# Two cross attentions: query scores directly behind mask and key scores, input transposes and query projection one period ahead

## The chip, the cores and the metric

The kernel runs on one core of a Trainium2 chip. The metric is device time in microseconds from the first to the last work of the program. Five engines work beside each other, each through its own queue in order: TensorE (PE, matrix multiplies), VectorE (DVE), ScalarE (ACT), GpSimd (POOL) and SyncE (SP, which here only issues transfers). They wait for one another by semaphores.

## The reference, cut to what matters

A decoder of two layers over 16 sequences of 256 rows of 256 numbers. Each layer is a mixer, a cross attention and a mixture of experts. The change touches only the two cross attentions. What one computes (16 heads of 16 numbers; the one of layer 0 has a mask):

```
q = x @ Wq.T + bq;  k = ctx @ Wk.T + bk;  v = ctx @ Wv.T + bv     # ctx has 256 rows as well
scores = einsum('bhqd,bhkd->bhqk', q, k) / sqrt(16)
scores = where(mask == 0, -1e9, scores)                           # layer 0 only
out = einsum('bhqk,bhkd->bhqd', softmax(scores), v)
x = layernorm(x + out @ Wo.T + bo)
logits = x @ router.T                                             # then top 2 of 7, or top 4 of 32
```

## The kernel before, in words

`xattn_stage` is built once for each layer. One sequence n is a unit of work; it passes through stages, and a *period* p works on several sequences at once: q = p is in its first pass over the scores, k = p-1 and l = p-2 in the second pass and the output, r = p-3 in the routing, and a = p+1 is being projected. `at(n, part, g)` issues a part if the sequence exists. The order in each engine's queue is written out by hand in the loops `for p in PERIODS`.

The softmax needs the maximum of each row first. So the scores are computed twice, in eight groups g of four heads by 128 rows:

- `query_scores(q, g)` (Q below; `x_ps<-x_kpack,x_qpack`, four matmuls on 48 of the array's rows) gives scores with the queries on the partitions. VectorE's `maxima(q, g)` takes the row maxima, in layer 0 with four custom operations that also add the mask (L1170), in layer 1 with one reduction (L1174). There is one buffer in PSUM, so Q of the next group waits for these maxima.
- `turn_maxima` (L912, `x_nmx`) transposes the finished maxima of all groups into the first bank of the same buffer; ScalarE's `keep_maxima` takes them negated, and SP's `pack_maxima` copies them as a 49th row beside the queries. Q of the next sequence waits until ScalarE has taken them.
- `key_scores(k, g)` (K; `x_ps<-x_qpack,x_kpack`, 49 rows) gives the transposed scores less the maximum. In layer 0 two matmuls with the mask (M, L892) go first. ScalarE's `weights` takes the exponential (L1068). `weigh` (W, L931, 16 matmuls) multiplies it with the values, `turn_output` (L943) transposes the result, VectorE's `scaled` divides it (L1181, L1183), `turn_scaled` (L851) and `output` (L954) project it, VectorE's `add_output` (L1191) adds it and takes the statistics, `normalize` (L206) ends it.

The queries and keys of sequence a are projected by `project_queries` and `project_keys` (L857), with the values' `project_values` (L883); the rows must first be transposed by `turn_in` (L851). All of these share one bank. ScalarE's `keep_queries` and `keep_keys` take them as a rounded part (`qh`, `kh`) and in full; GpSimd's `low_queries` (L803) and `low_keys` (L808) make the rest (`ql`, `kl`); SP packs both with six transfers each into `qpack` and `kpack`, which hold three sequences. GpSimd waits at each of these operations until VectorE is at a certain group of maxima: `beside_maximum`, group 2 for `low_queries`, 4 for `low_keys`, 5 for `add_bias` (L816).

The routing of r is `turn_rows` (L851), `route` (L970), VectorE's `take_logits`, `choose` (L1215 to L1226), `one_hot` (L1232 to L1240) and `weigh_experts` (L1246 to L1255), then `rank` on TensorE (L979 to L982) and `place` on VectorE. In layer 1 GpSimd also sends the rows out by indirect transfers (L826), four behind `low_queries` and four at the end of the period.

Of the kernel before, what the change touches and what calls it, by code (L numbers as in the profile page):

```python
# [7 lines left out]
F32 = mybir.dt.float32  # L8
# [604 lines left out]
def xattn_stage(nc, st, d, layer):  # L613
# [15 lines left out]
    PACKS = 3  # L629
    LOWEST = -3e38  # L630
    PACK_DMAS = 12
    GROUPS = QUADS * TB
    SLOTS = (0, 2, 1, 3)
    with ExitStack() as ctx:
# [58 lines left out]
        cx_loaded = [sem(f"cx_loaded{u}") for u in range(U)]  # L693
        pack_loaded = [sem(f"pack_loaded{u}") for u in range(PACKS)]
        max_loaded = [sem(f"max_loaded{u}") for u in range(PACKS)]
# [21 lines left out]

        PERIODS = range(-1, B + 4)

# [4 lines left out]
        def _(sp):  # L724
# [22 lines left out]

            def pack(dst, n, part, src):
                for m in range(KC):
                    lo = 64 * m + DH * part  # L750
                    sp.dma_start(dst[lo:lo + DH, n % PACKS].bitcast(F32),
                                 src[:, m, :].bitcast(F32)).then_inc(pack_loaded[n % PACKS], 16)

            def pack_queries(n):
                if n >= PACKS:
                    sp.wait_ge(st_ready, GROUPS * (n - PACKS + 1))
                sp.wait_ge(qh_ready, n + 1)
                pack(qpack, n, 0, qh)
                pack(qpack, n, 1, qh)
                sp.wait_ge(ql_ready, n + 1)  # L760
                pack(qpack, n, 2, ql)

            def pack_keys(n):
                if n < PACKS:
                    sp.wait_ge(ones_ready, n + 1)
                sp.wait_ge(kh_ready, n + 1)
                pack(kpack, n, 0, kh)
                pack(kpack, n, 2, kh)
                sp.wait_ge(kl_ready, n + 1)
                pack(kpack, n, 1, kl)  # L770

# [20 lines left out]
        def _(pool):  # L792
# [5 lines left out]
            def low_queries(n):  # L798
                pool.wait_ge(qh_ready, n + 1)
                if n:  # L800
                    pool.wait_ge(pack_loaded[(n - 1) % PACKS], 16 * PACK_DMAS * ((n - 1) // PACKS + 1))
                beside_maximum(n - 1, 2)
                pool.tensor_tensor(ql[:], qf[:], qh[:].bitcast(F32), ALU.subtract).then_inc(ql_ready, 1)  # L803

            def low_keys(n):
                pool.wait_ge(kh_ready, n + 1)
                beside_maximum(n - 1, 4)
                pool.tensor_tensor(kl[:], kf[:], kh[:].bitcast(F32), ALU.subtract).then_inc(kl_ready, 1)  # L808
# [37 lines left out]
        def _(pe):  # L846
# [53 lines left out]
            def query_scores(n, g):  # L900
                if g == 0:
                    pe.wait_ge(pack_loaded[n % PACKS], 16 * PACK_DMAS * (n // PACKS + 1))
                    if n:
                        pe.wait_ge(nmT_ready, n)
                if n or g:
                    pe.wait_ge(max_ready, GROUPS * n + g)
                scores(QUERY, n, g, qpack, kpack, 3 * DH, False).then_inc(s_ready, 1)
# [76 lines left out]

            for p in PERIODS:
                a, q, k, l, r = p + 1, p, p - 1, p - 2, p - 3
                at(l, key_scores, 6)
                at(l, weigh, 2)
                at(a, turn_in)
                at(k, turn_maxima)  # L990
                at(l, key_scores, 7)
                at(q, query_scores, 0)

                at(a, project_queries)
                at(r, turn_rows)
                at(q, query_scores, 1)

                at(l, weigh, 3)
                at(k, key_scores, 0)
                at(r, route)  # L1000
                at(q, query_scores, 2)

                at(k, key_scores, 1)
                at(a, project_keys)
                at(l, turn_output)
                at(q, query_scores, 3)

                at(k, key_scores, 2)
                at(k, weigh, 0)
                at(q, query_scores, 4)  # L1010

                at(k, key_scores, 3)
                at(a, project_values)
                at(l, turn_scaled)
                at(q, query_scores, 5)

                at(k, key_scores, 4)
                at(l, output)
                at(r, rank)
                at(q, query_scores, 6)  # L1020

                at(k, key_scores, 5)
                at(k, weigh, 1)
                at(q, query_scores, 7)
            if masked:
# [4 lines left out]
        def _(act):  # L1030
# [8 lines left out]
            def keep_queries(n):  # L1039
                act.wait_ge(q_ready, n + 1)  # L1040
                if n:
                    act.wait_ge(pack_loaded[(n - 1) % PACKS], 16 * PACK_DMAS * ((n - 1) // PACKS + 1))
                for c in range(KC):
                    act.activation(qf[:, c, :], bank(PROJ)[:, c, :], ACT.Identity, bias=bqk[:, 0, c:c + 1], scale=1.0)
                for c in range(KC):
                    ins = act.activation(qh[:, c, :], bank(PROJ)[:, c, :], ACT.Identity, bias=bqk[:, 0, c:c + 1], scale=1.0)
                ins.then_inc(qh_ready, 1)

            def keep_keys(n):
                act.wait_ge(k_ready, n + 1)  # L1050
                for c in range(KC):
                    act.activation(kf[:, c, :], bank(PROJ)[:, c, :], ACT.Identity, bias=bqk[:, 1, c:c + 1], scale=1.0)
# [39 lines left out]

            for p in PERIODS:
                a, k, l, r = p + 1, p - 1, p - 2, p - 3
                at(l, weights, 6)
                at(l, keep_values, 2)
                at(a, keep_rows)
                at(k, keep_maxima)
                at(l, weights, 7)

                at(a, keep_queries)
                at(r, keep_normal)

                at(l, keep_values, 3)
                at(k, weights, 0)

                at(k, weights, 1)
                if not masked:
                    at(r, gates)
                at(a, keep_keys)  # L1110

                at(k, weights, 2)
                at(k, keep_values, 0)

                at(k, weights, 3)
                if masked:
                    at(r, gates)
                at(l, keep_scaled)

                at(k, weights, 4)  # L1120

                at(k, weights, 5)
                at(k, keep_values, 1)

        @block.vector
        def _(dve):
# [151 lines left out]
            for p in PERIODS:  # L1278
# [15 lines left out]
                at(q, maxima, 6)  # L1294
                at(l, add_output)
# [994 lines left out]
```

## Time and profile before

| | |
|---|---|
| median of 3 runs | 3034.13 us (3027.97 to 3039.84) |
| the profiled execution: its own time, from its first to its last instruction (the span) | 3014.5 us; what lies around the span has no row |
| mean granted clock of TensorE over the span | 0.908 |
| busy: TensorE, VectorE, ScalarE, GpSimd | 2479.8, 1989.7, 1085.6, 829.1 us |
| cross attention of layer 0 | about 580 to 1068 us of the span |
| cross attention of layer 1 | about 2309 to 2790 us of the span |

Busy time is the sum of the durations of an engine's instructions. Matmuls overlap one another, so for TensorE the distances between the starts of groups tell more than the durations. "idle <- X" behind a row is the time in which the engine had nothing to run before it, and who released it. PEld are the weight loads that go before matmuls.

### The profile page before, as it was taken

What the parts mean: (1) busy time and instruction counts of PE and PEld (TensorE: products, weight loads), DVE (VectorE), ACT (ScalarE), POOL (GpSimd) and SP (SyncE); (2) the same over time, 40 slices, a digit from 0 to 9 for tenths busy, and PEclk for the clock granted to TensorE, in tenths of its full rate; (3) what the DMA queues carried; (4) which work ended last, traced back from release to release, by engine and by line L of the source; (5) the groups of instructions that cost most, each with busy time, mean ns of one, the idle gap of its engine ahead of it and who ended that gap; (6) DMA issues with size and microseconds to landing.
All of it is one profiled execution on the core that took longest, in us unless ns stands there. A gap on an engine that the chain in (4) does not pass through costs nothing. (4 is left out here: it accounts for less than half of the span.)

```text
span 3014.5 us, 50862 instructions
## 1 busy us (share of the span) xinstructions
PE 2479.8 (82%) x17441; PEld 2072.9 (69%) x17442; DVE 1989.7 (66%) x5320; ACT 1085.6 (36%) x1953; POOL 829.1 (28%) x1118
## 2 busy tenths in 40 slices
PE   3877887679999969999999999977675898887680
PEld 3666666546666569999999999966564566665670
DVE  5888888356776656566666666546553587886458
ACT  2333433235555522221222222212263555553450
POOL 0010001111111136223523213015311144444664
PEclk8998999879999979999999999988887898996895
DMA  1112213253544120001302202112102656550436
GB/s 56 50 49 67 78 49 117 46 78 68 110 68 75 23 91 35 28 31 64 112 31 70 70 28 70 34 52 58 35 0 45 83 99 125 78 76 3 128 110 246
DMA packets 170608, 206.04 MB, mean 68 GB/s; under 512 B 21061, under 2 KB 148847, under 8 KB 170480
## 3 DMA queue, kind: packets, MB, share of 16 engines
q1 hardware_dynamic: 139680, 154.58, 22.9%
q0 software_dynamic: 15360, 23.63, 2.7%
q10 hardware_dynamic: 15440, 26.22, 2.5%
q8 instruction: 69, 1.13, 0.2%
q14 instruction: 59, 0.48, 0.1%
HBM read 95.42 MB, written 77.20 MB: 57 GB/s over the span
## 5 line engine op out<-in xcount | busy, mean ns | idle before, releaser
L1538 PE MATMUL m_gu<-m_x_hi,m_w_hi 128*128 128x256 f32 x1632 | 461.1, 283 | 17.9 <-issue 10.4
L1538 PE MATMUL m_gu<-m_x_hi,m_w_lo 128*128 128x256 f32 x1632 | 457.7, 280 | 0.0
L1538 PE MATMUL m_gu<-m_x_lo,m_w_hi 128*128 128x256 f32 x1632 | 457.2, 280 | 0.0
L1575 ACT ACTIVATE m_sg<-m_gu 128x256 f32<-128x256 f32 x408 | 156.8, 384 | 668.7 <-PE m_gu L1538 668.7
L1609 DVE TENSOR_TENSOR m_h<-m_sg,m_gu 128x256 f32<-128x256 f32 x408 | 171.7, 421 | 286.6 <-ACT m_sg L1575 284.0
L1068 ACT ACTIVATE x_pt<-x_ps 128x1024 f32<-128x1024 f32 x256 | 262.0, 1024 | 224.5 <-PE x_ps L896 221.3
L1538 PEld LDWEIGHTS m_gu<-m_x_hi,m_w_hi 128*128 128x128 f32 x1632 | 308.9, 189 | 22.0 <-issue 11.8
L1538 PEld LDWEIGHTS m_gu<-m_x_lo,m_w_hi 128*128 128x128 f32 x1632 | 308.8, 189 | 0.0
L1538 PEld LDWEIGHTS m_gu<-m_x_hi,m_w_lo 128*128 128x128 f32 x1632 | 308.6, 189 | 0.0
L1170 DVE CUSTOM_DVE_ANT_0 x_ps<-x_ps,x_mb 128x256 f32<-128x256 f32 x512 | 201.7, 457 | 118.6 <-PE x_ps L896 118.5
L1527 PE MATMUL m_yp<-m_w_hi,m_h_hi 128*128 128x256 f32 x816 | 240.1, 294 | 5.1 <-DVE m_h_lo L1611 4.6
L1527 PE MATMUL m_yp<-m_w_lo,m_h_hi 128*128 128x256 f32 x816 | 230.2, 282 | 0.0
L1527 PE MATMUL m_yp<-m_w_hi,m_h_lo 128*128 128x256 f32 x816 | 229.3, 281 | 0.0
L1611 DVE TENSOR_TENSOR m_h_lo<-m_h,m_h_hi 128x256 fp32r<-128x256 f32 x408 | 198.9, 488 | 14.3 <-DVE m_h_hi L1610 0.4
L1174 DVE TENSOR_REDUCE x_nmx<-x_ps 128x4 f32<-128x1024 f32 x128 | 156.0, 1218 | 74.4 <-PE x_ps L896 73.9
L369 PE MATMUL rw_ps<-rw_mix,rw_fk 128*128 128x256 f32 x512 | 146.2, 456 | 56.8 <-DVE rw_mix L477 56.8
L896 PE MATMUL x_ps<-x_kpack,x_qpack 48*128 48x256 f32 x1024 | 135.3, 344 | 67.0 <-DVE x_nmx L1174 36.6
L369 PEld LDWEIGHTS rw_ps<-rw_mix,rw_fk 128*128 128x128 f32 x512 | 118.5, 235 | 82.0 <-DVE rw_mix L477 60.8
L896 PEld LDWEIGHTS x_ps<-x_kpack,x_qpack 48*128 48x128 f32 x1024 | 82.5, 198 | 125.2 <-DVE x_nmx L1174 55.3
L1527 PEld LDWEIGHTS m_yp<-m_w_hi,m_h_hi 128*128 128x128 f32 x816 | 154.0, 189 | 10.3 <-DVE m_h_lo L1611 7.4
L1455 POOL CAST m_w_hi<-raw 128x256 fp32r<-128x256 f32 x168 | 64.3, 432 | 343.4 <-DMA raw<-in_L_ffn_w_down 338.9
L188 POOL TENSOR_TENSOR rw_rstd<-rw_var,eps 128x2 f32<-128x2 f32 x48 | 11.2, 234 | 524.6 <-DVE rw_var L201 524.6
(314 smaller groups left out, 5718.2 us busy)
## 6 DMA issues: line engine op xcount, KB each, us to landing
yt<-zero SPq DMA_DIRECT2D x8, 2048.0 KB, 10.3
x_qpack<-x_qh SPq DMA_DIRECT2D x128, 128.0 KB, 4.0
x_kpack<-x_kh SPq DMA_DIRECT2D x128, 128.0 KB, 4.2
m_yr<-yt SPq DMA_DIRECT2D x16, 1024.0 KB, 13.3
m_x<-xs SPq DMA_DIRECT2D x36, 256.0 KB
ys<-m_y SPq DMA_DIRECT2D x35, 256.0 KB, 2.2
xs<-zero SPq DMA_DIRECT2D x8, 1072.0 KB, 5.9
m_x<-xs SPq DMA_DIRECT2D x32, 268.0 KB, 3.2
```

What stands on the lines that cost most here:

```text
L188: pool.tensor_tensor(rstd[:, u, :], var[:, u, :, 1], st.eps[:, 0:TB], ALU.add).then_inc(eps_added, 1)
L369: ins = pe.matmul(bank(u, m // 2)[:, m % 2, :], fk[:, c, m * P:m * P + P], mix[:, u, 0, c, :], start=(c == 0), stop=(c == KC - 1))
L896: ins = pe.matmul(bank(first + k // 2)[:, k % 2, :], left[here, n % PACKS, blk, t * P:t * P + P], moving[here, n % PACKS, blk, :], start=n ...
L1068: act.activation(pt[:, j % 2, t].rearrange("p k q -> p (k q)"), ps[:, KEY:KEY + 2].rearrange("p k q -> p (k q)"), ACT.Exp, scale=SCALE).th ...
L1170: ins = dve.tensor_tensor_reduce(row, row, mb[:, 0, t, :], op0=ALU.add, op1=ALU.max, scale=1.0, scalar=LOWEST, accum_out=nmx[:, n % U, t, ...
L1174: ins = dve.tensor_reduce(nmx[:, n % U, t, 0:HEADS].rearrange("p (m q b) -> p m q b", m=2, q=QUADS)[:, :, j, :], ps[:, QUERY:QUERY + 2].re ...
L1455: pool.tensor_copy(w_hi[:, b, n, piece], raw[:, n, piece]).then_inc(hi_ready, 1)
L1527: ins = pe.matmul(yp[:, n, 0:D], hp[:, m, n * P:n * P + P], wp[2][:, m, :], start=(m == 0 and k == 0), stop=(m == FC - 1 and k == 2))
L1538: ins = pe.matmul(gu[:, m % 4, n, :], wp[n][:, c, m * P:m * P + P], xp_[:, c, :], start=(c == 0 and k == 0), stop=(c == KC - 1 and k == 2))
L1575: act.activation(sg[:, m % 4, :], gu[:, m % 4, 0, :], ACT.Silu).then_inc(silu_ready, 1)
L1609: s.do(dve.tensor_tensor(h[:, m % 4, :], sg[:, m % 4, :], gu[:, m % 4, 1, :], ALU.mult))
L1611: dve.tensor_tensor(h_lo[:, m, :], h[:, m % 4, :], h_hi[:, m, :].bitcast(F32), ALU.subtract).then_inc(h_ready, 1)
```

## The change

On TensorE, `query_scores` of group g now stands directly behind `key_scores` of another group in all eight blocks of a period (before, other work stood between some of them). `turn_in` and `project_queries` work on b = p+2 instead of a = p+1, so there is one more period at the start. `turn_maxima` moves from the beginning of the next period to the end of its own. `project_keys`, `route`, `turn_output`, `turn_scaled`, `output`, `rank` and `project_values` change their blocks. The orders on ScalarE and VectorE follow; on VectorE `choose` moves behind `scaled`, and `values` ahead of maxima 5. Since queries are now packed in another period than keys, the one semaphore for both packs becomes two with six transfers each, and the waits on it are split; `keep_keys` and `low_keys` get a wait for the keys' pack of the sequence before.

```diff
-    PACK_DMAS = 12
+    PACK_DMAS = 6
...
-        pack_loaded = [sem(f"pack_loaded{u}") for u in range(PACKS)]
+        qpack_loaded = [sem(f"qpack_loaded{u}") for u in range(PACKS)]
+        kpack_loaded = [sem(f"kpack_loaded{u}") for u in range(PACKS)]
...
-        PERIODS = range(-1, B + 4)
+        PERIODS = range(-2, B + 4)
...
             def low_keys(n):
                 pool.wait_ge(kh_ready, n + 1)
+                if n:
+                    pool.wait_ge(kpack_loaded[(n - 1) % PACKS], 16 * PACK_DMAS * ((n - 1) // PACKS + 1))
                 beside_maximum(n - 1, 4)
...
             def query_scores(n, g):
                 if g == 0:
-                    pe.wait_ge(pack_loaded[n % PACKS], 16 * PACK_DMAS * (n // PACKS + 1))
+                    pe.wait_ge(qpack_loaded[n % PACKS], 16 * PACK_DMAS * (n // PACKS + 1))
+                    pe.wait_ge(kpack_loaded[n % PACKS], 16 * PACK_DMAS * (n // PACKS + 1))
...
             for p in PERIODS:
-                a, q, k, l, r = p + 1, p, p - 1, p - 2, p - 3
+                b, a, q, k, l, r = p + 2, p + 1, p, p - 1, p - 2, p - 3
                 at(l, key_scores, 6)
+                at(q, query_scores, 0)
                 at(l, weigh, 2)
-                at(a, turn_in)
-                at(k, turn_maxima)
+                at(r, turn_rows)
+
                 at(l, key_scores, 7)
-                at(q, query_scores, 0)
-
-                at(a, project_queries)
-                at(r, turn_rows)
                 at(q, query_scores, 1)
+                at(a, project_keys)
+                at(r, route)
+
+                at(k, key_scores, 0)
+                at(q, query_scores, 2)
                 at(l, weigh, 3)
-                at(k, key_scores, 0)
-                at(r, route)
-                at(q, query_scores, 2)
 
                 at(k, key_scores, 1)
-                at(a, project_keys)
+                at(q, query_scores, 3)
+                at(a, project_values)
                 at(l, turn_output)
-                at(q, query_scores, 3)
 
                 at(k, key_scores, 2)
+                at(q, query_scores, 4)
                 at(k, weigh, 0)
-                at(q, query_scores, 4)
+                at(l, turn_scaled)
 
                 at(k, key_scores, 3)
-                at(a, project_values)
-                at(l, turn_scaled)
                 at(q, query_scores, 5)
+                at(l, output)
+                at(b, turn_in)
 
                 at(k, key_scores, 4)
-                at(l, output)
+                at(q, query_scores, 6)
+                at(b, project_queries)
                 at(r, rank)
-                at(q, query_scores, 6)
 
                 at(k, key_scores, 5)
+                at(q, query_scores, 7)
                 at(k, weigh, 1)
-                at(q, query_scores, 7)
+                at(q, turn_maxima)
...
             def keep_keys(n):
                 act.wait_ge(k_ready, n + 1)
+                if n:
+                    act.wait_ge(kpack_loaded[(n - 1) % PACKS], 16 * PACK_DMAS * ((n - 1) // PACKS + 1))
...
                 at(l, weights, 6)
                 at(l, keep_values, 2)
-                at(a, keep_rows)
-                at(k, keep_maxima)
+                at(r, keep_normal)
+
                 at(l, weights, 7)
-
-                at(a, keep_queries)
-                at(r, keep_normal)
-
+                at(a, keep_keys)
+
+                at(k, weights, 0)
                 at(l, keep_values, 3)
-                at(k, weights, 0)
 
                 at(k, weights, 1)
                 if not masked:
                     at(r, gates)
-                at(a, keep_keys)
 
                 at(k, weights, 2)
                 at(k, keep_values, 0)
+                at(l, keep_scaled)
 
                 at(k, weights, 3)
                 if masked:
                     at(r, gates)
-                at(l, keep_scaled)
+                at(b, keep_rows)
 
                 at(k, weights, 4)
+                at(b, keep_queries)
 
                 at(k, weights, 5)
                 at(k, keep_values, 1)
+                at(q, keep_maxima)
...
                 at(q, maxima, 0)
                 at(r - 1, place)
                 at(q, maxima, 1)
+                at(q, maxima, 2)
                 at(r, take_logits)
-                at(q, maxima, 2)
-                at(r, choose)
                 at(q, maxima, 3)
                 at(l, scaled)
+                at(r, choose)
                 at(q, maxima, 4)
+                at(a, values)
+                at(q, maxima, 5)
                 at(r, one_hot)
-                at(q, maxima, 5)
-                at(a, values)
+                at(q, maxima, 6)
                 at(r, weigh_experts)
-                at(q, maxima, 6)
                 at(l, add_output)
                 at(q, maxima, 7)
```

## Rows read from the trace of the kernel before

**Rows 1.** Stretches (length; busy PE, PEld, DVE, ACT, POOL; clock, DMA share, GB/s); layer 0, 1

```profile
685.27:978.34 293.07, 291.41 (x2321) 185.86 (x2322) 205.08 (x1033) 163.76 (x276) 51.88 (x55) 1.00 0.47 82
2424.31:2739.03 314.72, 278.11 (x2308) 198.68 (x2308) 256.08 (x575) 174.74 (x291) 146.55 (x150) 0.90 0.55 87
2424.31:2449.02 24.71, 21.69 (x195) 15.67 (x195) 21.29 (x49) 14.91 (x26) 8.76 (x9) 1.00 0.53 98
2473.94:2500.88 26.94, 24.38 (x197) 17.56 (x196) 21.61 (x49) 15.08 (x26) 12.81 (x13) 0.88 0.58 93
```

**Rows 2.** TensorE in order of time, layer 0 (start us, us, engine, line, operation)

```profile
828.93 1.04 PE L943 MATMUL x_ps<-ident,x_o 128*128 128x128 f32 x8
829.90 0.50 PE L896 MATMUL x_ps<-x_kpack,x_qpack 48*128 48x256 f32 x4
...
831.30 1.07 PE L931 MATMUL x_ps<-x_pt,x_vp 128*32 128x256 f32 x16
832.30 0.50 PE L896 MATMUL x_ps<-x_kpack,x_qpack 48*128 48x256 f32 x4
832.74 0.60 PE L892 MATMUL x_ps<-x_mb,identb 128*128 128x512 bf16 x2
833.27 0.50 PE L896 MATMUL x_ps<-x_qpack,x_kpack 49*128 49x256 f32 x4
833.70 1.99 PE L883 MATMUL x_ps<-x_wv,x_cx 128*128 128x256 f32 x8
835.53 0.60 PE L851 MATMUL x_ps<-ident,x_aq 128*128 128x128 f32 x4
836.06 0.51 PE L896 MATMUL x_ps<-x_kpack,x_qpack 48*128 48x256 f32 x4
```

**Rows 3.** Weight loads in order of time where K and Q adjoin, layer 0

```profile
818.47 0.20 PEld L912 LDWEIGHTS x_ps<-ident,x_nmx 128*128 128x128 f32 x2 [0.38 <-DVE x_nmx L1170]
...
819.27 0.30 PEld L896 LDWEIGHTS x_ps<-x_qpack,x_kpack 49*128 49x128 f32 x4 [0.42 <-issue]
...
819.50 0.31 PEld L896 LDWEIGHTS x_ps<-x_kpack,x_qpack 48*128 48x128 f32 x4
...
819.94 0.19 PEld L857 LDWEIGHTS x_ps<-x_xT,x_wqk 128*128 128x128 f32 x1
```

**Rows 4.** VectorE in order of time, end of a period, layer 0

```profile
840.15 0.43 DVE L1170 CUSTOM_DVE_ANT_0 x_ps<-x_ps,x_mb 128x256 f32<-128x256 f32 x1 [0.83 <-PE x_ps L896]
...
843.44 0.41 DVE L1170 CUSTOM_DVE_ANT_0 x_ps<-x_ps,x_mb 128x256 f32<-128x256 f32 x1
```

**Rows 5.** VectorE's choose, then GpSimd's low_keys, layer 0

```profile
827.74 0.24 DVE L1220 MAX8 x_mx<-x_lg 128x8 f32<-128x8 f32 x2
...
828.42 0.14 DVE L1226 TENSOR_TENSOR x_tmp<-x_mx 128x2 f32<-128x2 f32 x1
...
832.96 1.27 POOL L808 TENSOR_TENSOR x_kl<-x_kf,x_kh 128x512 fp32r<-128x512 f32 x1 [5.30 <-PE x_ps L896]
```

**Rows 6.** GpSimd's low_queries, low_keys and VectorE's cast, layer 1

```profile
2535.30 1.27 POOL L803 TENSOR_TENSOR x_ql<-x_qf,x_qh 128x512 fp32r<-128x512 f32 x1 [2.22 <-PE x_ps L896]
...
2541.55 1.29 POOL L808 TENSOR_TENSOR x_kl<-x_kf,x_kh 128x512 fp32r<-128x512 f32 x1
2541.96 0.93 DVE L1232 CAST rows<-x_ix 128x8 f32<-128x8 uint32 x1
```

**Rows 7.** VectorE and GpSimd in the tail of layer 1

```profile
2748.86 1.83 DVE L1217 TENSOR_TENSOR x_lg<-x_sc,ebias 128x64 f32<-128x64 f32 x1
...
2749.31 1.29 POOL L816 TENSOR_TENSOR x_y<-rows,x_rows 128x512 f32<-128x512 f32 x1
```

**Rows 8.** Stretches of VectorE's work, layer 1: maxima 0, place, 1; choose; weigh_experts to add_output

```profile
2529.49:2533.68 4.19, 4.19 (x37) 2.92 (x37) 3.95 (x9) 2.70 (x7) 2.91 (x3) 1.00 0.29 74
2536.60:2538.63 2.03, 2.03 (x20) 1.73 (x18) 1.65 (x10) 1.31 (x4) 1.60 (x2) 1.00 1.02 310
2546.83:2551.47 4.64, 2.87 (x44) 1.41 (x42) 4.24 (x14) 2.28 (x3) 0.00 (x0) 0.95 1.13 174
```

More of the change, by code:

```diff
@@ L746, in load_context, with pack @@
                     sp.dma_start(cx[:, n % U], ctx_v[:, :, S * n:S * n + S]).then_inc(cx_loaded[n % U], 16)
-            def pack(dst, n, part, src):
+            def pack(dst, n, part, src, loaded):
                 for m in range(KC):
@@ L751, in pack @@
                     sp.dma_start(dst[lo:lo + DH, n % PACKS].bitcast(F32),
-                                 src[:, m, :].bitcast(F32)).then_inc(pack_loaded[n % PACKS], 16)
+                                 src[:, m, :].bitcast(F32)).then_inc(loaded[n % PACKS], 16)
             def pack_queries(n):
@@ L757, in pack_queries @@
                 sp.wait_ge(qh_ready, n + 1)
-                pack(qpack, n, 0, qh)
-                pack(qpack, n, 1, qh)
+                pack(qpack, n, 0, qh, qpack_loaded)
+                pack(qpack, n, 1, qh, qpack_loaded)
                 sp.wait_ge(ql_ready, n + 1)
-                pack(qpack, n, 2, ql)
+                pack(qpack, n, 2, ql, qpack_loaded)
             def pack_keys(n):
@@ L766, in pack_keys @@
                 sp.wait_ge(kh_ready, n + 1)
-                pack(kpack, n, 0, kh)
-                pack(kpack, n, 2, kh)
+                pack(kpack, n, 0, kh, kpack_loaded)
+                pack(kpack, n, 2, kh, kpack_loaded)
                 sp.wait_ge(kl_ready, n + 1)
-                pack(kpack, n, 1, kl)
+                pack(kpack, n, 1, kl, kpack_loaded)
             def pack_maxima(n):
@@ L800, in low_queries @@
                 if n:
-                    pool.wait_ge(pack_loaded[(n - 1) % PACKS], 16 * PACK_DMAS * ((n - 1) // PACKS + 1))
+                    pool.wait_ge(qpack_loaded[(n - 1) % PACKS], 16 * PACK_DMAS * ((n - 1) // PACKS + 1))
                 beside_maximum(n - 1, 2)
@@ L1041, in keep_queries @@
                 if n:
-                    act.wait_ge(pack_loaded[(n - 1) % PACKS], 16 * PACK_DMAS * ((n - 1) // PACKS + 1))
+                    act.wait_ge(qpack_loaded[(n - 1) % PACKS], 16 * PACK_DMAS * ((n - 1) // PACKS + 1))
                 for c in range(KC):
@@ L1093, in _ @@
             for p in PERIODS:
-                a, k, l, r = p + 1, p - 1, p - 2, p - 3
+                b, a, q, k, l, r = p + 2, p + 1, p, p - 1, p - 2, p - 3
                 at(l, weights, 6)
                 at(l, keep_values, 2)
-                at(a, keep_rows)
-                at(k, keep_maxima)
+                at(r, keep_normal)
                 at(l, weights, 7)
-                at(a, keep_queries)
-                at(r, keep_normal)
+                at(a, keep_keys)
+                at(k, weights, 0)
                 at(l, keep_values, 3)
-                at(k, weights, 0)
                 at(k, weights, 1)
```

## The prediction, made before the changed kernel had run

> **What bounds the kernel now.** First I read the busy time of the engines in the two cross attention stages, by stretches [rows 1]. Of eleven full periods of the first stage (each one sequence of 256 rows; 293.07 us, so 26.64 us a period) TensorE is busy 291.41 us at full clock, VectorE 205.08: TensorE bounds it. In the second stage a clean period takes 24.71 us, and VectorE, busy 21.29 us of it, is the tighter engine. [...] The twelve full periods take 314.72 us, 26.23 on average.
>
> A busy TensorE says little about its peak, so next I read its order of time [rows 2]. Its slots are the distances between starts: transposing the output 0.97 us (O8, 828.93 to 829.90), weighing 1.00 (W, from 831.30), query scores 0.44 (Q, 832.30), mask 0.53 (M), key scores 0.43 (K), a projection 1.83 (P, from 833.70), four small transposes 0.53 (T, 835.53 to 836.06). For routing (R, eight matmuls) I take O8's 1.0, for the five placement matmuls of `rank` .2, both estimates. There is no gap in the first stage but before the transpose of the maxima.
>
> Third, the one place of the old order where K and Q stand side by side [rows 3]: weight loads start at 819.27 (K), 819.50 (Q), 819.94 (projection). The pair takes 0.67 us, not 0.43 + 0.44 = 0.87.
>
> **The change, part by part.** *Pairs.* In the masked stage K is followed by Q once a period today, and eight times after: 7 x 0.20 = 1.4 us less TensorE work a period [rows 2, 3]. The period's TensorE work goes from 26.64 - 0.27 (the wait before the maxima's transpose, 0.80 between it and T instead of 0.53; its idle shows at 818.47 [rows 3]) = 26.37 to 24.95. In the unmasked stage Q and the next K already adjoin where no other work stands between, seven times a period, so only one pair is won: 0.2 us.
>
> *Where the saving goes.* `turn_maxima` needs all eight maxima. Today the next period's first M, K, W and `turn_in` lie between Q7 and it (2.5 us); after, one W (1.0). I count from Q6, layer 0. TensorE: Q .44 + P 1.83 + rank .2 + M .53 + K .23 + Q .44 + W 1.0 = 4.67 us. VectorE: .6 until the scores are read (GpSimd, which waits for the same scores, starts .66 behind Q4: 832.30 and 832.96 [rows 2, 5]; VectorE follows its work without a gap there), maxima 6 and `add_output` 3.29 (adjoining today: 840.15 to 843.44), `weigh_experts` about .56 (three tiny operations like 828.42's), maxima 7 until its transpose is released 1.67 (the same point a period before: 818.47 + 26.64 = 845.11): 6.12 us [rows 3, 4]. So TensorE stands 1.45 us, where it stood 0.27.
>
> *The middle of the period.* I lay the new order out by those slots, T=0 at the first M. Q2 falls at 7.51, Q3 at 9.78 (waits .07 for maxima 2), then P and O8 end at 13.02. `scaled` now precedes `choose` on VectorE and has to wait for O8: 13.16, ends 14.22 (its reciprocal and two products stand 1.06 apart from the next work in VectorE's order of time). `choose` takes .84, its last operation (828.42) begins .68 into it [rows 5], at 14.90. Meanwhile Q4 at 13.78 lets GpSimd's `low_keys` go .66 later (1.27 long [rows 5]): 14.44 to 15.71. The two overlap; today they don't. What does an overlap cost? Today a cast of 8 elements starts at 2541.96 and ends at 2542.89, just behind GpSimd's `low_keys` that ran from 2541.55 to 2542.84 [rows 6], where 828.42's kind takes .14 to .2. And in the tail of layer 1 a subtraction-sized VectorE operation with two inputs in SBUF took 1.83 us and ended when GpSimd's 2749.31 operation did [rows 7]. 828.42 also has two SBUF inputs. No row shows it blocked; the bounds are nothing and .8 us (until 15.77). I take the upper, since the nearest row is [rows 7].
>
> [...]
>
> Then maxima 4 start at 15.77 (else 15.06), Q5 1.67 later at 17.44 (16.73; TensorE would be there at 16.51), Q6 at Q5 + 1.83 + .53 + .44 + .76 = 21.0 (20.29), the transpose of the maxima at Q6 + 6.12 = 27.12 (26.41), and the next period .27 later: 27.39 us (26.68) against 26.64. So +.75 (+.04) a period. Eleven full periods: +8.3 (+.4). The first and last periods lack `choose` or projections; by the same walk they give back about 1. **Layer 0: +7 (-1) us.**
>
> *Layer 1, the same walk* with maxima that stand 1.14 apart when VectorE has them ready. Slots of VectorE: the two first maxima with `place` 4.19, so `place` 1.91; `choose` 2.03; `weigh_experts`, maxima 6 and `add_output` 4.64 [rows 8]. From the transpose of the maxima to Q0 stays about .93. The new waits of VectorE: place ends at 4.22, maxima 1 at 5.36; but Q2 is behind P, R and K0 (now that both stand in one block): 6.27, so maxima 2 start at 6.87: 1.5 us idle. Q3 at 8.14, O8 ends at 11.38, `scaled` waits until 11.52 (nearly 1.9 us behind maxima 3) and `choose` can't fill that, being behind it: 12.57. Its addition with two SBUF inputs comes .8 in, 13.37. GpSimd's `low_queries` starts about .68 behind Q2 (.66 in layer 0), four indirect DMAs follow, and `low_keys` starts 6.25 after it (2535.30, 2541.55 [rows 6]): 13.20 to 14.49. The addition waits until then: choose ends 15.54 (unblocked 14.60). Maxima 4, then Q5 at 16.81 (15.87), where TensorE is at 13.81; later it waits 2.3 more for the maxima's transpose. `add_bias` .66 behind Q5 runs to 18.74 (17.80) and holds back only the cast (.2); today it waits for `low_keys` [rows 6], and I take the same .75 for the later addition of `one_hot`, which today runs beside `add_bias`: `one_hot` shrinks by 1.4, to about 1.7. Q6 19.84 (18.90), maxima 6 from 20.44 (19.50), + 4.63 + 1.25 = transpose at 26.32 (25.38), next period .36 later: 26.68 (25.74) against 24.8, so +1.8 (+.9). Twelve periods: +22 (+10); the periods without projections or routing give back 3.5.
>
> *Clock.* Layer 1's twelve periods average 26.23 us where a clean one takes 24.8: 17 us in all, above all stretches at 1.2 GHz (the average clock is .90 [rows 1]). Today TensorE stands before Q6, Q7 and the maxima's transpose with no projection between; the new order waits more, but with a projection behind each of Q5 and Q6, so the waits are spread. I take a third, 6 us, back; bounds 0 and 17. **Layer 1: +22 - 3.5 - 6 = +12 (0).**
>
> *Hidden.* `turn_in` and `project_queries` a period ahead issue the same instructions and six DMAs; the first set runs while TensorE waits for the first key pack to land. The query packs start earlier on SP, ahead of the key packs, so nothing is queued behind them longer. ScalarE's and GpSimd's new waits for the last key pack are for one that landed a period ago (ScalarE is idle 9.8 of 24.71 us [rows 1]). `keep_queries` between weights 4 and 5 delays weights 5 by .5 us; M of the next period comes 1.3 us later. `pack_maxima` gains 2 us. Were that cover gone, each would cost its own length, .6 to 1.6 us a period.
>
> **Sum.** The profiled execution has a span of 3014.5 us; the runs' median, 3034.1, lies 19.6 above it, which I leave alone. 3034.1 + 7.3 + 12 = 3053 us. Around .5% (15 us) is what can be told from no change.
>
> **Rivals.**
> [...]
> *The saving is kept* (.10), the other side: if the VectorE work from Q6 to the transpose is hidden, TensorE's 24.95 us is the period. It decides at one point, a chain of less than 4.7 us there instead of 6.12. Against it: each term is measured. 11 x 1.42 + 1 + 3 for layer 1 = -20: 3014.
> *The clock falls oftener* (.13): more waiting in layer 1 puts 1.2 GHz into each of twelve periods at 2.2 us: 26 us instead of the 11 that the forecast leaves: 3053 + 15 = 3068. For it: TensorE stands 5 us of 26.7 instead of about 3. Against: the spread, and layer 0's full clock [rows 1] with stands shorter than layer 1's.
>
> **How the numbers follow.** Forecast .52, own range 3041 to 3064. With the rivals at .25, .10 and .13, the range 3026 to 3070 leaves out the kept saving and the worst clock. Slower by over .5% (above 3049): .34 from the forecast and .12 from the clock, .46. Faster (below 3019): .10 and .02 from no collision with all clock regained: .12. The same: .42.
>
> **What would show it.** M, K, Q to the next start in 1.20 us in layer 0; the transposes of the maxima 27.4 us apart (26.7 without the collision), with a wait of about 1.4 us for VectorE; L1226 taking .9 instead of .14; in layer 1, distances of 26.7, L1217 at about 1.2, L1232 and L1239 short, VectorE idle before maxima 2 and before L1181. It is wrong if the wait at L912 is short, if those two stay at .14 and .23, or if the clock in layer 1 changes much.

## The result, and the profile after

The changed kernel takes 3078.21 us (median of 4 runs, 3062.62 to 3086.43), the kernel before 3033.28 beside it: 1.015 times as long, with a 95% interval of 1.0107 to 1.0193. The forecast was 3053 with a range of 3026 to 3070: the direction was right, and the size outside the range. The names and operations are those of before; lines of `xattn_stage` stand 3 to 6 lines further down (L912 is now L916, L896 L899, L1170 L1176, L1174 L1180, L1217 L1223, L1226 L1232).

The span and clock of the profiled execution:

```profile
core 0: 3067.9 us, clock 0.900
```

Layer 0, TensorE in order of time; these answer to [rows 2]:

```profile
854.66 0.59 PE L895 MATMUL x_ps<-x_mb,identb 128*128 128x512 bf16 x2
855.18 0.50 PE L899 MATMUL x_ps<-x_qpack,x_kpack 49*128 49x256 f32 x4
855.52 0.40 PE L899 MATMUL x_ps<-x_kpack,x_qpack 48*128 48x256 f32 x4
855.85 1.07 PE L935 MATMUL x_ps<-x_pt,x_vp 128*32 128x256 f32 x16
...
865.13 0.50 PE L899 MATMUL x_ps<-x_kpack,x_qpack 48*128 48x256 f32 x4 [0.62 <-DVE x_nmx L1176]
...
874.70 0.44 PE L916 MATMUL x_ps<-ident,x_nmx 128*128 128x128 f32 x2 [1.45 <-DVE x_nmx L1176]
```

Mask, keys, queries to the next start take 1.19 us (854.66 to 855.85), the forecast's 1.20 against 1.40 before. The transpose of the maxima waits 1.45 us for VectorE, the forecast's 1.45 against 0.27. The first line below is VectorE's last operation of `choose`, the second GpSimd's `low_keys`; they answer to [rows 5]:

```profile
862.73 0.80 DVE L1232 TENSOR_TENSOR x_tmp<-x_mx 128x2 f32<-128x2 f32 x1
...
862.23 1.28 POOL L811 TENSOR_TENSOR x_kl<-x_kf,x_kh 128x512 fp32r<-128x512 f32 x1 [4.86 <-PE x_ps L899]
```

An operation on two elements of each partition, 0.14 us long before, takes 0.80 and ends when GpSimd's does: the collision of the forecast is there. Yet the transposes of the maxima stand only 26.91 us apart (847.79 to 874.70), not 27.39, and the 15 distances of layer 0 (632.60 to 1031.86) sum to 399.26 us against 396.02: the layer lost 3 us, not 7. Of these 3, one period (792.48 to 820.87, 28.39 us at a clock of 0.94) has 1.5; the other full periods add 0.27 each, and the second distance of the layer gives back 1.2 (24.67 against 25.89).

Layer 1, by stretches (columns as in [rows 1]): all 15 distances between transposes of the maxima, a long one, and one at full clock.

```profile
2363.26:2786.10 422.84, 355.74 (x2792) 249.76 (x2792) 289.78 (x644) 209.25 (x353) 158.28 (x162) 0.87 0.45 78
2492.16:2526.09 33.93, 28.96 (x196) 20.68 (x196) 21.46 (x49) 14.76 (x25) 12.76 (x13) 0.75 0.40 73
2646.81:2672.84 26.03, 21.93 (x195) 15.78 (x196) 20.09 (x49) 14.43 (x25) 12.71 (x13) 1.00 0.46 74
```

The same for the unchanged kernel, profiled a second time for this study (e11 below):

```profile
2356.80:2753.57 396.77, 345.87 (x2819) 243.19 (x2819) 287.30 (x644) 216.25 (x360) 158.14 (x162) 0.91 0.49 83
2590.79:2619.89 29.10, 24.73 (x197) 17.59 (x196) 19.60 (x48) 15.27 (x26) 12.28 (x13) 0.87 0.45 68
2619.89:2645.15 25.26, 22.15 (x196) 15.77 (x196) 20.03 (x49) 14.86 (x26) 12.74 (x13) 1.00 0.52 76
```

Layer 1 lost 26 us. A period at full clock is 26.03 us long against 25.26 here and 24.71 in [rows 1]. The mean clock is 0.87 against 0.91. Cut into stretches of 0.3 us, this layer of the changed kernel has a granted clock of 1.00 in 1019 of 1409 and of 0.50 in 361 (without a break from 2493.50 to 2502.50 us), e11 in 1065 and 234 of 1322: two levels, full and half, and few stretches with a mean between them. So 2 x 0.13 x 422.84 = 110 us are at half clock against 2 x 0.09 x 396.77 = 71. Where the prediction and the expectations give a clock in GHz, they mean the 0.50; no run shows a clock in GHz. Over the last twelve distances, changed kernel and e11:

```profile
2438.52:2786.10 347.58, 292.78 (x2301) 205.90 (x2301) 247.07 (x575) 169.15 (x286) 146.26 (x150) 0.87 0.44 78
2427.20:2753.57 326.37, 283.32 (x2308) 199.96 (x2308) 245.73 (x575) 173.30 (x291) 146.18 (x150) 0.91 0.47 83
```

These are some 90 and 59 us at half clock; [rows 1] have 2 x 0.10 x 314.72 = 63 for the first trace of the kernel before.

What TensorE does before the clock falls shows in a period at full clock. Behind each of these rows stands its wait; the last two lines are VectorE and GpSimd, answering to [rows 7]:

```profile
2663.38 0.50 PE L899 MATMUL x_ps<-x_kpack,x_qpack 48*128 48x256 f32 x4 [1.64 <-DVE x_nmx L1180]
...
2672.84 0.44 PE L916 MATMUL x_ps<-ident,x_nmx 128*128 128x128 f32 x2 [2.13 <-DVE x_nmx L1180]
...
2660.95 0.22 DVE L1223 TENSOR_TENSOR x_lg<-x_sc,ebias 128x64 f32<-128x64 f32 x1
...
2662.03 1.26 POOL L811 TENSOR_TENSOR x_kl<-x_kf,x_kh 128x512 fp32r<-128x512 f32 x1 [1.16 <-remote]
```

Two waits of 1.6 and 2.1 us stand in such a period, as forecast (it had 3.0 before Q5 and 2.3; the first is shorter since the addition L1223 takes 0.22 and is over before `low_keys` begins). In a period in which TensorE is late by a stretch at half clock the two do meet:

```profile
2510.33 1.31 DVE L1223 TENSOR_TENSOR x_lg<-x_sc,ebias 128x64 f32<-128x64 f32 x1
...
2510.26 1.29 POOL L811 TENSOR_TENSOR x_kl<-x_kf,x_kh 128x512 fp32r<-128x512 f32 x1
```

That happens four times (at 2510, 2543, 2576 and 2744 us), and these are the four longest periods, 33.93, 31.54, 31.02 and 30.78 us. In this trace that collision meets only periods that are late already. It is not what makes them long: in e6 below the addition takes 0.22 to 0.23 us throughout, and yet three full periods there are 31.3 to 31.7 us long; and in e7 it takes 1.41 us (at 2459.12) in a period of 26.90 us at full clock.

The waits over the twelve last distances (us in total, times, the longest), changed kernel:

```profile
DVE x_nmx L1180 <- PE x_ps L899: 58.8, 42, 4.4
...
PE x_ps L916 <- DVE x_nmx L1180: 30.2, 13, 3.1
...
PE x_ps L899 <- DVE x_nmx L1180: 22.9, 13, 2.7
```

and the kernel before (e11):

```profile
DVE x_nmx L1174 <- PE x_ps L896: 29.4, 39, 3.3
...
PE x_ps L896 <- DVE x_nmx L1174: 22.7, 27, 1.8
...
PE x_ps L912 <- DVE x_nmx L1174: 4.6, 7, 1.2
```

TensorE waits 53 us for maxima instead of 27, and VectorE 59 us for scores instead of 29. (With VectorE's waits for which the profile finds no releaser, which it calls "remote", 2.7 and 14.0 us, VectorE's are 62 and 43; more of these at e11.) Both engines stand more: neither is the bound of this order, their handing over is.

Between the two spans (3067.9 and 3030.3 in e11) the 37.6 us divide so: until the first transpose of layer 0 1.3, layer 0 3.3, from its last to the first of layer 1 1.9, layer 1 26.1, what follows 5.1. The medians lie some 7 us further apart than the two profiled spans; no trace shows where.

### The profile page after: what moved, and what is told of

The parts are those of the page before. It is cut to its first block and busy times, and to the rows that moved or that the text cites. A ratio compares the mean times of both kernels' runs of the same rounds, so it can differ in the third digit from the quotient of the medians.

```text
span 3067.9 us, 50898 instructions
## 1 busy us (share of the span) xinstructions
PE 2483.1 (81%) x17441; PEld 2084.1 (68%) x17442; DVE 1987.7 (65%) x5320; ACT 1081.6 (35%) x1953; POOL 829.7 (27%) x1118
## 5 line engine op out<-in xcount | busy, mean ns | idle before, releaser
L1176 DVE CUSTOM_DVE_ANT_0 x_ps<-x_ps,x_mb 128x256 f32<-128x256 f32 x512 | 201.6, 456 | 113.6 <-PE x_ps L899 113.6
L1180 DVE TENSOR_REDUCE x_nmx<-x_ps 128x4 f32<-128x1024 f32 x128 | 156.1, 1219 | 115.8 <-PE x_ps L899 106.5
L899 PE MATMUL x_ps<-x_kpack,x_qpack 48*128 48x256 f32 x1024 | 122.2, 319 | 61.3 <-DVE x_nmx L1180 31.1
L1533 PEld LDWEIGHTS m_yp<-m_w_hi,m_h_lo 128*128 128x128 f32 x816 | 153.8, 189 | 0.0
L1533 PEld LDWEIGHTS m_yp<-m_w_lo,m_h_hi 128*128 128x128 f32 x816 | 153.6, 188 | 0.0
```

What stands on the lines that cost most here:

```text
L899: ins = pe.matmul(bank(first + k // 2)[:, k % 2, :], left[here, n % PACKS, blk, t * P:t * P + P], moving[here, n % PACKS, blk, :], start=n ...
L1176: ins = dve.tensor_tensor_reduce(row, row, mb[:, 0, t, :], op0=ALU.add, op1=ALU.max, scale=1.0, scalar=LOWEST, accum_out=nmx[:, n % U, t, ...
L1180: ins = dve.tensor_reduce(nmx[:, n % U, t, 0:HEADS].rearrange("p (m q b) -> p m q b", m=2, q=QUADS)[:, :, j, :], ps[:, QUERY:QUERY + 2].re ...
L1533: ins = pe.matmul(yp[:, n, 0:D], hp[:, m, n * P:n * P + P], wp[2][:, m, :], start=(m == 0 and k == 0), stop=(m == FC - 1 and k == 2))
```

## The experiments

In the fragments A is the changed order and B that of before. Layer 0 is the masked one. "Layer 0" and "layer 1" below are the sums of the 15 distances between transposes of the maxima in the run's trace.

**e1 and e2: one layer each.** TensorE's, ScalarE's and VectorE's loops are A in one layer, B in the other; the two semaphores and the two new waits stay in both.

```
if masked:      # e1: A here, B below; e2: B here, A below
    for p in PERIODS: ...
else:
    for p in PERIODS: ...
```

> Layer 0 in the new order, layer 1 in the order of before. If the loss sits in layer 1 (my theory after the result: the trace after has 4 us of the 53 in layer 0), this is 3033 + 4 = 3037, with 26.92 us a period in layer 0 and layer 1's periods back at 24.8 clean, 26.2 on average. Rival, a loss that both layers share (the clock of the whole program, or the split semaphores): 3050 or more.

> Layer 1 in the new order, layer 0 in the order of before. Theory: 3033 + 38 = 3071 or so (3060 to 3080), clean periods of 26.05 us, most periods longer by a stretch at 1.2 GHz. Rival, a loss that needs both: under 3050.

e1: 3042.38 us (10 runs), 1.0037 (1.0019 to 1.0056) of before. Layer 0 has 26.91 us a period, 399.31 in all; layer 1, whose order is unchanged, 397.24. e2: 3073.59 us (5 runs), 1.0146 (1.0115 to 1.0177); layer 0 397.28, 26.70 a period; layer 1 419.20. The loss is in layer 1's order. The 397 us of an unchanged layer 1 in e1 seemed to cost 12 against the 385.17 of the trace I had read; e10 and e11 settle that.

**e3, e4, e7, e8: fill TensorE's waits.** Matmuls whose result nobody reads go in front of `weigh`, where TensorE waits anyhow in layer 1. They tell whether it is the standing that brings the lower clock.

```diff
+            def keep_warm(count):
+                for i in range(count):
+                    pe.matmul(bank(WEIGH)[:, 1, :], wqk[:, 0, 0, 0:P], wqk[:, 1, 0, :], start=True, stop=True)
...
             def weigh(n, j):
+                if not masked:
+                    keep_warm((6, 8, 0, 0)[j])    # e3 in A; e7 in A: (3, 4, 0, 0); in B: e4 (0, 8, 2, 0), e8 (0, 4, 1, 0)
```

> The new order in both layers; in layer 1 TensorE also runs 6 projection-sized matmuls into an unused half bank before weigh 0 and 8 before weigh 1 of each sequence, 14 of 0.21 us = 3.0 us a period, in the time in which it waits for VectorE before Q5 (1.6) and before the transpose of the maxima (2.1). If the stretches at 1.2 GHz come from TensorE's waits and make the loss, they go: twelve periods at 26.1 to 26.4 instead of 28.9, so 3078 - 30 = 3048 (3042 to 3056). Rival, the long periods are waits of VectorE or for transfers at whatever clock: they stay, and 3 us more TensorE work a period makes 3080 to 3110.

> The order of before in both layers; in layer 1 TensorE also runs 8 projection-sized matmuls before weigh 1 and 2 before weigh 2 (2.1 us a period), where it waits before Q7 and before the transpose of the maxima. By the clock theory the stretches at 1.2 GHz in layer 1 go, twelve periods of 24.9 to 25.1 instead of 26.2: 3033 - 14 = 3019 (3015 to 3026). Rival, clock not caused by the waits: 3033 or up to 3050 for the added work.

e3: 3086.27 us (1.0191, 1.0157 to 1.0225), layer 1 428.83. e4: 3072.09 (1.0146, 1.0115 to 1.0178), layer 1 423.00. Each matmul cost 0.46 us, twice what I had meant, so the added work was longer than the waits and the totals say nothing of the clock. But its own column does: in layer 1 it is 0.97 and 0.98, and e3's full periods are nearly even (28.3 us, two at 29.2 and 29.6), where those of the changed kernel range from 26.03 to 33.93. Hence the same with half as many:

> As e3_after_filled with half the added matmuls: each of them shows as two of the trace and takes .46 us, so 3 and 4 of them are 1.4 and 1.8 us, inside the waits of 1.6 and 2.1 us. Clock theory: the clock of layer 1 stays at full after its first periods, all twelve full periods at 26.1 to 26.5 us, whole 3078 - 28 = 3050 (3045 to 3060). Rival, that the long periods are not the clock's doing: 28.9 on average stays.

> As e4_before_filled with half the added matmuls: 4 before weigh 1 (1.8 us) and 1 before weigh 2 (.5 us), in the order of before. Clock theory: layer 1 at full clock, 24.9 to 25.2 us a period, 3031 - 13 = 3018. Rival: no change, 3031, or slower by the added 2.3 us a period if the waits can't take them: up to 3060.

e7: 3059.26 us (6 runs, 1.0086, 1.0061 to 1.0112), some 19 below the changed kernel though it does more. Its layer 1, a long period in it and a plain one:

```profile
2366.19:2772.69 406.50, 370.67 (x3001) 264.34 (x3001) 288.66 (x644) 209.75 (x353) 158.21 (x162) 0.96 0.50 81
2608.15:2636.31 28.16, 25.06 (x210) 18.18 (x210) 21.55 (x49) 14.41 (x26) 12.77 (x13) 1.00 0.53 71
2636.31:2663.08 26.77, 25.05 (x209) 18.17 (x210) 20.19 (x49) 14.54 (x26) 12.74 (x13) 1.00 0.48 72
```

TensorE is busy 3.1 us more in a period, and layer 1 is 16.3 us shorter (406.50 against 422.84; e2 and e5, with the same order there, have 419.20 and 426.25), at full clock in every full period but the last. All six runs of e7 have a mean clock of 0.913 to 0.915 and times of 3054.92 to 3061.56 us, all four of the changed kernel 0.896 to 0.904 and 3062.62 to 3086.43. A period costs 26.8 instead of 26.0, which was expected at 26.1 to 26.5, so the whole came at the upper end of its 3045 to 3060. That the standing brings the lower clock (0.87 over layer 1, 0.96 with the waits filled), and that this costs layer 1 some 13 to 20 us, is shown. That the collisions went away is no rival: e7 has three in its last twelve distances. The long period shown has one of them, though its clock is full; the first operation of `choose` takes 1.64 us there instead of the 0.18 of the changed kernel:

```profile
2622.16 1.64 DVE L1227 TENSOR_SCALAR x_sc<-x_sc 128x64 f32<-128x64 f32 x1
...
2622.43 1.31 POOL L811 TENSOR_TENSOR x_kl<-x_kf,x_kh 128x512 fp32r<-128x512 f32 x1
```

e8: 3051.54 (9 runs, 1.0057, 1.0039 to 1.0075), where 3018 was expected: a clear miss. In the old order the clock rises too (0.95), but layer 1 goes from 396.77 (e11; 395.37 in e10, which has the split semaphores as e8 has) to 401.09: TensorE waits less there (27 us for maxima over the twelve distances of e11, against 53), and the added work lengthens the period.

**e5, e6, e9, e12: VectorE's order.** e5, in layer 0 only, moves `choose` back in front of `scaled`, away from `low_keys`, and takes `add_output` and `weigh_experts` out of the chain from Q6 to the transpose of the maxima. e6 moves only `choose`, in both layers.

```diff
-                at(l, scaled)
                 at(r, choose)
+                at(l, scaled)
...
+                at(l, add_output)
                 at(q, maxima, 6)
-                at(r, weigh_experts)
-                at(l, add_output)
                 at(q, maxima, 7)
+                at(r, weigh_experts)
```

> The changed kernel, with VectorE's order changed in layer 0 alone: choose before scaled, add_output before maxima 6, weigh_experts behind maxima 7. Theory (the chain of VectorE from Q6 to the transpose of the maxima and the collision in choose took the saving of layer 0): with choose first Q5 comes .8 earlier, and the wait before the transpose falls from 1.45 to .9; so 25.4 to 25.5 us a period in layer 0 instead of 26.92, about 17 us over the layer. Whole: 3078 - 17 = 3061. Rival, TensorE's own order holds the period: 26.9 stays.

> The changed kernel with choose before scaled on VectorE in both layers, nothing else. Theory: layer 0 loses the collision of choose with low_keys and the wait before Q5: 26.0 us a period instead of 26.92 (L1232 back at .14). Layer 1's clean periods go from 26.05 to about 25.3, since choose fills VectorE's wait for turn_output; part is given back where the cast of one_hot meets add_bias. Rival: the place of choose is without weight, both stay.

e5: 3056.78 us (10 runs, 1.0087, 1.0063 to 1.0111), 25.31 us a period, layer 0 380.95 instead of 399.26, as expected. The saving of the pairs was real, and VectorE's chain and the collision held it back. e6: 3058.63 us (6 runs, 1.0093, 1.0058 to 1.0127), layer 0 26.02 a period as expected, 388.54 in all. The collision is gone from it (L1232 takes 0.14), while the wait before the transpose of the maxima is still there:

```profile
869.08 0.44 PE L916 MATMUL x_ps<-ident,x_nmx 128*128 128x128 f32 x2 [1.44 <-DVE x_nmx L1176]
```

So of the 1.60 us a period between the changed kernel and e5, the place of `choose` with its collision has 0.89 (26.91 to 26.02), and the tail of VectorE 0.71 (26.02 to 25.31). With `choose` alone moved the layer is 7 us faster than before.

In layer 1 e6 has 416.43 us at the same mean clock of 0.87, without a collision in the addition: 6.4 less than the changed kernel, of which the third distance has 4.1 (24.18 at full clock, where it was 28.24 at 0.94). A clean period was to fall to 25.3 and has 26.15:

```profile
2701.89 1.23 DVE L1180 TENSOR_REDUCE x_nmx<-x_ps 128x4 f32<-128x1024 f32 x1 [1.01 <-remote]
```

```profile
2699.42 0.40 PE L899 MATMUL x_ps<-x_kpack,x_qpack 48*128 48x256 f32 x4
...
2702.90 0.50 PE L899 MATMUL x_ps<-x_qpack,x_kpack 49*128 49x256 f32 x4 [1.31 <-ACT x_pt L1074]
```

VectorE is ready for maxima 4 at 2700.9, and by its row Q4 (2699.42) is over at 2699.8; yet VectorE starts at 2701.89 and ScalarE's next exponential at 2701.83, and for neither does the profile name a releaser. TensorE then waits 1.31 for that exponential. The gain is lost there, and what holds the two engines is open.

e9 puts e5's layer 0 beside a layer 1 exactly as before, with one semaphore for both packs there.

> Layer 0 has the changed order on TensorE and ScalarE with VectorE's order moved as in the run e5_tail_moved; layer 1 is exactly as in the kernel before, with one semaphore for both packs. Theory (VectorE's chain held layer 0's saving back, and layer 1's loss comes only from layer 1's own order): layer 0 at 25.3 us a period, 381 us for its 15 distances against 396; layer 1 as before at 385 us, give or take 8 for where its 1.2 GHz stretches fall; in all some 3017 us, 15 below the kernel before, between 3008 and 3028. Rival (a faster layer 0 changes the state in which the clock's record reaches the later stages, so that they give the gain back, as the run e1_layer0_only had layer 1 at 397 us with its order unchanged): layer 1 at 397 us and the whole at 3028 to 3034, no faster than before.

e9: 3016.11 us (8 runs, 3010.16 to 3022.76) against 3031.45 (19 runs): 0.9947, 0.9928 to 0.9967. **This version beats both kernels.** Its two layers, and the end of a period of layer 0:

```profile
632.87:1013.75 380.88, 362.07 (x3028) 240.13 (x3028) 273.66 (x1357) 213.99 (x352) 67.55 (x71) 0.97 0.46 77
2343.52:2740.20 396.68, 345.25 (x2820) 242.84 (x2820) 288.51 (x644) 215.79 (x360) 158.13 (x162) 0.91 0.49 83
```

```profile
862.03 0.44 PE L917 MATMUL x_ps<-ident,x_nmx 128*128 128x128 f32 x2 [0.73 <-DVE x_nmx L1253]
```

Layer 0 gives 15.1 us; layer 1 has the 397 us of the expectation's rival and the whole the time of its theory, since 397 is what the unchanged kernel takes there as well (396.77 in e11). The rest of VectorE's chain still costs TensorE 0.73 us a period.

e12 asks whether VectorE's order alone would have done it: in the kernel before, only `add_output` goes in front of maxima 6 and `weigh_experts` behind maxima 7, in layer 0.

> The kernel before, with one edit in layer 0: on VectorE add_output goes in front of maxima 6 and weigh_experts behind maxima 7, as in the run e9_tail_moved_layer0_only, while TensorE's and ScalarE's order stay as before. It tells whether that run's 25.3 us a period comes from the pairs on TensorE or from VectorE's order alone. Theory (the old order is bound by TensorE, with a wait of .27 us before the maxima's transpose as all that VectorE could give back): 26.4 us a period, 11 x .25 = 3 us in all, 3029. Rival (VectorE's order alone brings it): 25.3 us a period and the whole at 3016.

e12: 3040.07 us (8 runs, 1.0028, 1.0011 to 1.0046), 27.59 us a period, layer 0 408.23. Slower, which neither theory had.

```profile
845.06 0.50 PE L896 MATMUL x_ps<-x_kpack,x_qpack 48*128 48x256 f32 x4
...
848.59 0.50 PE L896 MATMUL x_ps<-x_kpack,x_qpack 48*128 48x256 f32 x4 [1.06 <-DVE x_nmx L1170]
```

```profile
845.13 0.69 DVE L1191 TENSOR_TENSOR x_y<-x_y,x_ps 128x512 f32<-128x512 f32 x1 [0.71 <-PE x_ps L954]
```

In the old order `output` stands right in front of Q6, so `add_output` waits for it and holds maxima 6 back, and Q7, whose turn comes 2.5 us behind Q6, waits 1.06 for them. The move pays in e9, where the new order has put `output` a block earlier, and costs here. With VectorE's tail the same, the rest of the new order (TensorE's, ScalarE's and the earlier part of VectorE's) is worth 27.59 - 25.31 = 2.28 us a period, of which the pairs are at most 1.4.

**e10 and e11: what the split costs, and what the kernel before really takes.** e10 has B in both layers and of the change only the two semaphores and the two new waits. e11 is the kernel before, profiled again.

> Both layers in the order of the kernel before; of the change only the two separate pack semaphores and the two new waits (keep_keys, low_keys). Theory (waits that are met when they are reached cost next to nothing): layer 0 at 26.70 us a period against 26.64, as the run e2_layer1_only had it, +1 us; layer 1 385 us; in all 3034, between 3029 and 3039. Rival (the split itself made layer 1 longer in the run e1_layer0_only, 397 us against 385): layer 1 near 397 us and the whole at 3042 to 3048.

> The kernel before, unchanged, profiled a second time, because its first profiled execution (span 3014.5 us) was shorter than every one of the 22 unprofiled runs beside the later experiments. Theory (that execution was a lucky one, and layer 1's time in the old order is some 395 us as in the three runs e1_layer0_only, e9_tail_moved_layer0_only and e10_split_only): layer 0 again 396 us for its 15 distances, layer 1 393 to 399, span 3022 to 3035. Rival (an unchanged kernel really has 385 us in layer 1, and each of those edits cost about 10): layer 1 at 383 to 388, span 3012 to 3018.

e10: 3035.53 us (10 runs), 1.0012 (0.9997 to 1.0028), layer 0 at 26.70 a period, layer 1 395.37. e11: 3029.87 (8 runs), 0.9988 (0.9972 to 1.0004); layer 0 396.00, layer 1 396.77, span 3030.3. The split costs 0.06 us a period and nothing that the whole can tell. Every further trace with the old order in layer 1 (e1, e9, e10, e11, e12) has 392 to 397 us there; the 385.17 of the first trace stands alone. Its clock is not the reason (63 us at half clock in the twelve distances, 59 in e11). What differs is a wait in the middle of the period, here in e11:

```profile
2494.07 0.50 PE L896 MATMUL x_ps<-x_kpack,x_qpack 48*128 48x256 f32 x4 [0.39 <-DVE x_nmx L1174]
...
2496.64 1.22 DVE L1174 TENSOR_REDUCE x_nmx<-x_ps 128x4 f32<-128x1024 f32 x1 [1.56 <-remote]
...
2496.58 0.39 ACT L1075 ACTIVATE x_o<-x_ps 128x256 f32<-128x256 f32 x1 [2.00 <-remote]
...
2496.75 1.26 POOL L808 TENSOR_TENSOR x_kl<-x_kf,x_kh 128x512 fp32r<-128x512 f32 x1 [1.34 <-remote]
```

```profile
DVE x_nmx L1174 <- remote: 14.0, 9, 1.7
```

Three engines stand until the same moment, 2 us behind the end of Q4 by its row, and the profile finds no instruction that released them. In e11 maxima 4 wait so in nine of the twelve periods, 14.0 us in all; e9, e10, e12 and e1 have such waits too (12 to 18 us), and the first trace has none. What causes them is open.

## Why the forecast was right in its direction and wrong in its size

I forecast 19 us more and 45 were measured. Of the 25 that lie between, layer 0 has 4 the other way (3 instead of 7), layer 1 has 14 (26 instead of 12), 8 lie outside the two layers and 7 between spans and medians. Within layer 1 the errors have both signs: the periods at full clock came out 7 to 13 us better than forecast, the first periods 8 worse, and what lies beyond clean periods 12 to 18 worse. Some of the size is thus luck: with full-clock periods as long as I had them the miss would have been larger.

- **Pairs: right.** 1.19 us for mask, keys, queries and the next start; 0.20 won a pair.
- **The wait that takes the saving: right in place and size.** 1.45 us before the transpose of the maxima. With the collision already gone (e6, 26.02 a period), e5 and e9 halve this wait (0.73) and the period falls to 25.31.
- **The collision in layer 0: right.** L1232 0.80: the operation starts behind GpSimd's (862.73 against 862.23) and ends at 863.5, with it. In [rows 7] VectorE's row starts first (2748.86 against 2749.31), and it is still VectorE's operation that is long (1.83 us) and lasts to GpSimd's end. The same in e7 (2622.16 against 2622.43, 1.64 us). So by these rows an operation of VectorE that starts up to 0.45 us ahead is not spared. I gave "no collision" a chance of .25, as an estimate of mine; in layer 1 of the changed kernel the addition was spared where it was over before `low_keys` began (0.22 us long from 2660.95, `low_keys` from 2662.03).
- **Layer 0's period: the mechanism right, the size off.** I forecast +0.75 us and measured +0.27. The difference lies in front of Q5, which comes 17.07 us behind the first mask (848.06 to 865.13), not 17.44; from Q5 to Q6 it is 3.57 where I had 3.56, and from Q6 to the transpose 6.00 (868.70 to 874.70), not 6.12. Half of the 0.37 in front of Q5 comes from TensorE: Q4 stands 13.59 behind the first mask, not 13.78, since I had costed slots in front of a mask as those in front of scores (`turn_output` 0.88, 859.91 to 860.79, where [rows 2] have 0.97; the transposes of the rows 0.49, 850.33 to 850.82, not 0.53). The rest is the hand-over: `low_keys` starts 0.58 behind Q4 (861.65, 862.23), not 0.66, and maxima 4 (863.45) 0.06 ahead of its end, where I had them 0.06 behind. +3 us for the layer, not +7, though one period at a lower clock, which I had not counted, brought 1.5 of the 3.
- **Layer 1 at full clock: the mechanism right, half the size.** +0.8 to +1.2 us a period (26.03 against 25.26, or the 24.8 of the forecast), not +1.8. The upper of two bounds failed here: `low_keys` starts a microsecond behind the addition, so the value without the collision (+0.9) holds in its three periods at full clock. 12 periods: about +9 to +15, not +22.
- **The first periods: missed.** I gave back 3.5 us there; the first three distances came out 4.9 us longer than e11's, nearly all in the third (28.24 against 23.23). In it `low_keys` (2423.04) meets the first operation of `choose` (1.08 us instead of 0.18), TensorE waits 2.54 us in front of Q5, and behind that the clock falls (0.94 over the period). In e6, with `choose` first, this distance is 24.18 at full clock.
- **Clock: the step that failed.** "I take a third, 6 us, back." Taking 26.03 and, for before, 24.8 to 25.26 as a clean period, what the twelve full periods have beyond clean ones is 347.58 - 12 x 26.03 = 35 us after and 23 to 29 in e11: 6 to 12 us more, not 6 less. The time at half clock in these distances is 90 us where it was 59 (63 in the trace I had read), half as much again instead of a third less. That waits with a projection behind them would cost less clock was my assumption, which no row of the kernel before shows, and they did not. e7 shows the cause: fill the same waits, and the clock in those periods is 1.00 and layer 1 16.3 us shorter. So the rival "the clock falls oftener", which I gave .13, was what came (its 2.2 us a period are the 26.94 at a clock of 0.88 less the 24.71 at 1.00 of [rows 1]). The collision of layer 1 that I had counted in every period came in four of twelve, and e6 has the lower clock without it.
- **The base.** I read 17 us beyond clean periods, most of it the clock's, from one execution; e11 has 29 by the same clean 24.8, with as much time at half clock (59 us against 63). The other 12 go with the waits without a named releaser: at the same mean clock of 0.96 a period of e11 with such a wait takes 26.11 us, and those of the first trace 24.84 to 24.97. One profile could not tell me so, though a span 19.6 us below the median was the hint that I left alone.
- **Small slips.** 26.68 against 24.8 is +1.9, not +1.8, and twelve times 0.94 is 11, not 10; and were TensorE's 24.95 us the period, each would gain 1.69, not 1.42, so that rival stands at 3011, not 3014. None changes the forecast by more than 1 us.
- Beyond the two layers 8 us went: ahead of layer 0's first transpose of the maxima 1.3, between the two layers' transposes 1.9, and behind layer 1's last one 5.1. I had nothing for these, and what causes them is open.

## What to carry to other kernels

Before paying for a denser order on one engine, walk the chain of the other engine that closes the loop, and move its work in the same edit: here the same pairs on TensorE lost 3 us in layer 0 with VectorE's order of the change, won 7 with `choose` back in front of `scaled`, and 15 with `add_output` and `weigh_experts` out of the chain as well. Where two engines hand buffers back and forth, read waits in both directions: if both grow, the order is worse even if it saves work. And judge a stage whose time varies between executions by several traces, not one: an untypical execution looks like a property of the kernel.

## What the runs showed that I had not expected

- Waits of 1.6 and 2.1 us in a period in which TensorE is busy 21.9 of 26.0 us went with a mean clock of 0.69 to 0.94 in nine of the last twelve distances, while useless matmuls in the same places kept it at 1.00 in eleven of them and made layer 1 16.3 us shorter.
- One fp32 matmul of the program with 256 columns cost 0.46 us and appears as two in the trace (7 added, 14 more records a period in e7).
- GpSimd's `low_keys` and VectorE's cast behind it [rows 6] overlapped in most periods of the first trace of the unchanged kernel (0.93 us) and in one of e11's (0.27 in the others), where both engines stand waiting ahead of it, with no releaser named: the phase of two engines differs between executions of one program.
